# A two-layer early-fusion transformer: exponentials taken straight from the score banks in the second layer

## What is computed

```python
# second layer, attention (x is the normed h, 69 x 256 for each sample)
scores = einsum('bhqd,bhkd->bhqk', q, k) * 16 ** -0.5
scores = where(causal, scores, -inf)
weights = softmax(scores, axis=-1)
h = h + einsum('bhqk,bhkd->bhqd', weights, v) @ c_proj_w + c_proj_b
# second layer, feed-forward (x is the normed h again)
y = bit_linear(x, w1)                 # 256 -> 1024, per-token scale 127/max|x|, rounded
y = silu(depthwise_conv1d(y))         # three taps along the tokens
h = h + bit_linear(y, w2)             # 1024 -> 256, per-token scale from max|y|, rounded
```

## Time and profile before

| | |
|---|---|
| device time, median of 3 runs | 857.08 us (856.58 to 857.84) |
| the profiled execution | 857.1 us, its span on the core 855.3 us |
| PE busy in the span | 754.5 us (88%) |
| DVE busy | 596.7 us (70%) |
| ACT busy | 439.1 us (51%) |
| POOL busy | 381.2 us (45%) |
| granted TensorE clock, mean | 0.932 |

### The profile page before, as it was taken

How to read it: one execution, slowest core, us unless ns; L and a number is a source line. 1 busy time by engine, 2 the same in 40 slices (tenths; PEclk the granted TensorE clock), 3 DMA queues, 4 the chain that set the end, 5 groups by cost and what they waited for, 6 DMA issues and landing times.

```text
span 855.3 us, 20374 instructions
## 1 busy us (share of the span) xinstructions
PE 754.5 (88%) x6953; PEld 667.5 (78%) x6953; DVE 596.7 (70%) x1446; ACT 439.1 (51%) x1047; POOL 381.2 (45%) x515
## 2 busy tenths in 40 slices
PE   4999999999999961999993999999999999999533
PEld 4999999999999950676663998888888888888322
DVE  0467777767777747222221358999999999999893
ACT  1444554444454431222221567777777777776551
POOL 1434545445545542222204676666666666652000
PEclk8999999999999975899996899999999999999755
DMA  5365321000000422222210000000000000000000
GB/s 172 97 250 214 59 61 24 12 9 9 8 14 10 155 17 48 45 68 62 69 51 20 7 15 9 7 16 15 15 16 15 16 15 17 16 9 11 7 7 14
DMA packets 23983, 36.41 MB, mean 43 GB/s; under 512 B 10038, under 2 KB 21211, under 8 KB 23115
## 3 DMA queue, kind: packets, MB, share of 16 engines
q1 hardware_dynamic: 14474, 26.20, 10.8%
q0 software_dynamic: 5808, 5.63, 3.1%
q10 hardware_dynamic: 3600, 3.28, 1.1%
HBM read 27.21 MB, written 7.88 MB: 41 GB/s over the span
## 4 chain that ended last, share of the span: by engine, by line
PE 57%; DVE 24%; issue 11%; DMA 4%; ACT 2%; POOL 1%; SPq 1%; DVEq 0%; ACTq 0%; POOLq 0%
PE bank_h L1494 5%; PE bank_d L1494 4%; PE bank_f L1468 4%; PE bank_e L1468 4%; PE bank_b L1456 4%; PE bank_g L1479 4%; PE bank_e L1649 3%; PE bank_c L1505 3%; PE bank_c L1667 3%; PE bank_c L1445 3%; PE bank_f L1649 2%; DVE diff L908 2%; PE bank_d L1667 2%; DVE w L1207 2%; PE bank_a L1445 2%
## 5 line engine op out<-in xcount | busy, mean ns | idle before, releaser
L466 POOL TENSOR_TENSOR qbd<-qt,consts_f 128x560 f32<-128x560 f32 x128 | 163.8, 1286 | 186.2 <-PE bank_e L1468 94.9
L615 ACT ACTIVATE pt<-bank_g 69x448 f32<-69x448 f32 x128 | 69.3, 541 | 35.5 <-PE bank_h L1479 34.1
L609 ACT ACTIVATE prob<-diff 112x345 f32<-112x345 f32 x128 | 62.0, 485 | 38.7 <-DVE diff L908 38.7
L1494 PE MATMUL bank_h<-values,pt 69*69 69x68 f32 x1024 | 74.5, 226 | 2.2 <-ACT pt L624 2.2
L1468 PEld LDWEIGHTS bank_e<-kt,qbd 128*112 128x112 f32 x640 | 71.7, 179 | 1.4
L1494 PEld LDWEIGHTS bank_d<-values,pt 69*69 69x69 f32 x1024 | 70.5, 143 | 2.2
L1468 PEld LDWEIGHTS bank_f<-kt,qbd 128*112 128x112 f32 x640 | 72.1, 180 | 0.0
L1494 PEld LDWEIGHTS bank_h<-values,pt 69*69 69x69 f32 x1024 | 70.0, 142 | 2.6 <-ACT pt L615 2.5
L1479 PE MATMUL bank_g<-consts_f,prob 112*69 112x112 f32 x512 | 71.9, 263 | 0.0
L1494 PE MATMUL bank_d<-values,pt 69*69 69x68 f32 x1024 | 71.8, 226 | 0.0
L1468 PE MATMUL bank_f<-kt,qbd 128*112 128x69 f32 x640 | 71.7, 260 | 0.0
(11 more groups left out here) (208 smaller groups left out, 1877.3 us busy)
## 6 DMA issues: line engine op xcount, KB each, us to landing
w<-in_w SPq DMA_DIRECT2D x2, 4096.0 KB, 14.4
patches<-in_patches SPq DMA_DIRECT2D x16, 222.0 KB, 2.6
expert_results<-prob ACTq DMA_DIRECT2D x25, 128.0 KB, 1.9
expert_rows<-x SPq DMA_DIRECT2D x16, 138.0 KB
out<-h SPq DMA_DIRECT2D x16, 138.0 KB
f_raw<-in_f SPq DMA_DIRECT2D x2, 1024.0 KB, 8.5
patches<-in_b SPq DMA_DIRECT2D x1, 2048.0 KB, 9.6
wqkv<-in_wqkv SPq DMA_DIRECT2D x2, 768.0 KB
```

Of the source, the lines that this page charges most:

```text
L466: pool.tensor_tensor(qbd[u % 2][:], q.broadcast_to([128, NG, HPB, QG]), head_mask.unsqueeze(1).unsqueeze(3).broadcast_to([128, NG, HPB, QG ...
L609: act.activation(prob[u % 2][:], diff[u % 2][:], ACT.Exp, scale=DH ** -0.5).then_inc(S["prob_made"], 1)
L615: act.activation(pt[u % 2][:, :, 0:4, :].rearrange("t h g q -> t g h q"), banks["g"][0:T, 0:4 * SR].rearrange("t (g h q) -> t g h q", g=4, ...
L1494: ins = mm(heads_out[b][:, hd * (DH + 1):(hd + 1 + AHEAD) * (DH + 1)], pt[u % 2][:, i, :, :].rearrange("k g q -> k (g q)")[:, 0:T], values ...
```

## The change

Four things change, nearly all in the second layer.

1. **Sign.** `head_mask` carries -1/4 in place of 1 and the mask +1e30 in place of -1e30, in both layers, so the banks hold the scores negated and scaled. DVE takes the row minimum in place of the maximum (`row_min`, the same instruction with another operation), and the exponential's scale is -1. The first layer keeps `shift_scores` and one exponential of 345 columns.
2. **No shift in the second layer.** `shift_scores` is gone there. `exp_rows` takes the place of `exp_scores`: ACT reads the bank itself, one instruction for each of the five query groups, with that group's row minimum as per-partition bias. Group g covers only its causal keys, 14, 28, 42, 56 and 69 columns. The bank is free, and PE's `turn_p` may start, when the last of the five is done.
3. **Zeros.** Columns of `prob` beyond the causal ones are no longer written, so DVE clears both `prob` tiles once between the layers, after the last expert rows are stored; the first exponential waits for that.
4. **Orders.** The four bodies of the second layer are written in other orders with other lags (largest lag 7 in place of 6 on PE and DVE, 4 in place of 3 on POOL), and `BANKS1` with them. PE's instructions are the same in kind and number, and so are all others but those named above.

```diff
+            def exp_rows(p, u):
+
+                bank = "ef"[u % 2]
+                act.wait_ge(S["min_made"], UNITS * p + u + 1)
+                wait(act, S["p_turned"], UNITS * p + u - 1)
+                if p == 0 and u == 0:
+                    act.wait_ge(prob_cleared, 2)
+                sc = banks[bank][0:SR, 0:NG * T].rearrange("r (g k) -> r g k", g=NG)
+                for g in range(NG):
+                    n = min(T, QG * (g + 1))
+                    ins = act.activation(prob[u % 2][:, g, 0:n], sc[:, g, 0:n], ACT.Exp,
+                                         scale=-1.0, bias=rowmin[:, u % 2, g:g + 1])
+                ins.then_inc(BK[bank], 1)
...
-                dve.tensor_reduce(rowmax[:, u % 2, :], sc, X, ALU.max).then_inc(S["max_made"], 1)
+                dve.tensor_reduce(rowmin[:, u % 2, :], sc, X, ALU.min).then_inc(S["min_made"], 1)
...
+            for k in range(2):
+                dve.wait_ge(y_stored[k], 16 * ((TILES - k + 1) // 2))
+                dve.memset(prob_t[k][0:SR, :], 0.0).then_inc(prob_cleared, 1)
...
-                if live(s, 2, PAIRS):
-                    shift_scores(s - 2, 0)
-                    row_max(s - 2, 1)
...
             def turn_p(p, u):
-                pe.wait_ge(S["prob_made"], UNITS * p + u + 1)
+                if S is LS[0]:
+                    pe.wait_ge(S["prob_made"], UNITS * p + u + 1)
+                else:
+                    bank_is_moved("ef"[u % 2], f"scores{u}", p)
...
-            steps(pe, PAIRS, 6, body1)
+            steps(pe, PAIRS, 7, body1)
...
-    head_mask=_p[:, None] // DH == np.arange(HPB)[None, :],
+    head_mask=-(DH ** -0.5) * (_p[:, None] // DH == np.arange(HPB)[None, :]),
```

291 lines of the change are left out of this document (145 added, 146 removed).

## The result

The changed kernel takes 861.65 us (median of 7 runs, 860.47 to 864.55) beside 857.08 for the kernel before on the same chip (median of 7 runs, 855.75 to 861.17): ratio 1.0057, 95% interval 1.0036 to 1.0078. It is 0.6% slower where 1.3% faster was forecast, and outside the range. Its profiled execution took 862.7 us, 5.6 more than that of before.

A forecast was written before the change was run, and what follows sets the result against it. DVE was taken as the bound (21.05 of 21.09 us a step), PE close behind. Terms +1.5 - 2.3 - 9.4 - 2.0 + 1 = -11.2 us from 857.1 gave 845.9, say 846.0 us, 1.3% faster; range 842 to 853.5.

The forecast's parts named there:

- DVE loses the shifts: Second layer: four shifts a pair go, 1.8 us, so DVE's step falls to 19.3 us, under PE's floor by 0.8.
- the ten steps: Pairs 3 to 13: each step 0.94 us shorter at 20.15, together -9.4 us (ends -10.1 and -7.0).
- if POOL's spread queries run late: Condition in the rival that orders don't quite fit: step 20.5 to 20.9 us, 849.3 to 853.3 us, chance 0.17.
- no gain: Rival: waits held by DVE's shifts turn up elsewhere, as in the scores chain; step 21.0 to 21.1, 857 us, chance 0.07.
- PE's floor of 20.1: Full step: PE needs 20.1 us once its two waits for DVE are gone, so PE is late next.
- 0.9 a unit: ACT's five short exponentials take 0.9 us per unit, making 18.6 us a pair (17.8 to 20.2), under PE's 20.1.
- The start: Up to the first projection: 2.1 us delay plus about 1 allowance less 1.7 given back, +1.5 us (ends 0 and +4).
- Pairs 0 to 3: Steps between their projections: PE's work listed at 52.3 us in place of 54.6, so -2.3 us (ends 0 and -3).
- a PE with more gaps: Allowance of about 1 us for the delay at the first scores, with no row for it.
- Pairs 13 to 15: Between their add_projected: 19.8 plus 17.7, together 37.5 us in place of 39.5, so -2.0 us (ends -0.5 and -2.7).
- the drain: After pair 15's add_projected: 53.0 us before; left_tap ahead of scale_gated delays the output product, +1 us (ends -0.5 and +2).
- Slower: Rival that ACT becomes the bound: short exponentials don't overlap, ACT's step 22.4 us, about 872 us, chance 0.09.

The follow-up runs named there:

- pool_narrow: Changed kernel with POOL's mix and bias additions narrowed to 2 of 256 columns a batch, leaving out most of both sums; 844.92 us in one run.
- covered: fitted with DVE's x_diagonal and z_unscale moved up behind x_round, and variance2 with add_ffn put ahead of gate_hidden; 853.21 us, ratio 0.9968.
- mix_narrow: Changed kernel with only POOL's mix narrowed to 2 of 256 columns of each sample; 853.07 us in one run.
- before_narrow: Kernel before with POOL's mix and bias additions narrowed to 2 of 256 columns; 855.09 us in one run.
- small_moved: Changed kernel with DVE's x_unscale moved right behind x_scale, and z_step and x_step ahead of right_tap; 855.28 us, ratio 0.9975.
- fitted: bias_later with DVE's add_right and x_round moved behind add_projected and the row minimum of unit 2; 858.25 us, ratio 1.0027.
- bias_later: small_moved with POOL's bias addition moved from the start of its step to behind the gather of expert results; 851.39 us, ratio 0.9952.
- before_provoked: Kernel before with POOL's bias addition moved up right behind the gather of expert results; 877.13 us in one run.

## Why the prediction was wrong, point by point

**DVE loses the shifts, its step falls to 19.3.** This is the step that failed, and not in its arithmetic. DVE's own work did fall, to 19.0 (pool_narrow). But the durations were taken from rows of the kernel before, and the new orders gave three of those operations another neighbour on POOL: 2.4 us a step. So the ten steps came out at +3.3 where -9.4 was forecast. The prediction asked of the orders only what each item waits for by semaphore. It checked POOL for lateness ("if POOL's spread queries run late"), not for what runs on DVE beside it. That an idle engine's work can be a cost to the bound engine was in none of its rivals: "no gain" came near in time, 857, with a mechanism (the chain of scores) that no run shows. What stands ahead of the prediction says that the engines meet only at semaphores; DVE and POOL meet here without one. (A slip without weight: the ten steps between projections are 21.09 on the mean, but go from 21.06 to 21.23.)

**PE's floor of 20.1** was right: 20.02 with the short additions, 19.93 in covered. The gain of ten steps that it promised was 9.4; pool_narrow has 200.2 us for the ten, 10.7 less than before.

**ACT** was right: 0.9 a unit, ACT 18.9 in a step of after with everything, against 18.6. The Trainium skill, page ScalarE: Activation LUTs, section What ACT_TABLE_LOAD costs, makes 1.1 a unit by its rule (the prediction's estimate); the trace has 0.91. The clearing lay inside DVE's idle time, as said.

**The start** was right in its first two parts; its sum cannot be judged from one profile. The first norm starts at 462.49 (462.3 was worked out), `move_xt` at 464.78 (464.6). But the first projection came at 491.73. Stretches of before and after in that place:

```profile
472.00:480.00 8.00, 7.90 (x48) 7.91 (x49) 2.08 (x4) 3.45 (x10) 3.56 (x4) 0.57 0.07 18
```

```profile
472.00:480.00 8.00, 8.00 (x81) 7.39 (x80) 2.67 (x6) 7.10 (x28) 6.03 (x7) 1.00 0.01 2
```

Before, PE ran at a clock of 0.57 there, after at 1.00; so a faster PE made up for the delay of 2 us. That is no effect of the new orders that could be counted on: mix_narrow and pool_narrow have the same orders as after, and there the clock was 0.63 and 0.69 in this stretch and the first projection came at 495.67 and 494.20. And before_narrow has the orders of the kernel before, a clock of 1.00 there, and its first projection at 491.00. With a low clock in this stretch the kernels with new orders have it between 494.2 and 496.3, near the forecast's 496.

**Pairs 0 to 3:** -2.3 forecast, +5.0 measured. The list of PE's work was too short by 1.3 to 1.8 us, as pool_narrow (53.6, -1.0) and covered (54.1, -0.5) show with the clock at 1.00, where 52.3 was forecast. The rest is the low clock, for which the prediction had an allowance at the start ("a PE with more gaps") and nowhere else. It followed two PE waits of 0.84 and 0.85 us. The second is for the diagonal, which stood on DVE behind an `x_unscale` held for 1.0 us at 528. In small_moved `x_unscale` is short there, but `add_right` is held in its place (2.17), and PE waits 0.85 us for the diagonal as well; its other wait is 0.21, the clock stays at 1.00 and the three pairs take 54.2. So it is not shown that the hold-up brought the low clock. Against it speaks that in before_narrow, where DVE's operations ahead of the wait have their bare times, pairs 0 to 3 took 58.7 us with the same low clock. In both stretches its clock is much like that of after; up to pair 3 it takes 549.74 us and after 551.35, so with like clocks these two terms together cost 1.6 us, where -0.8 was forecast.

**Pairs 13 to 15** (-2.0) and **the drain** were right: between the additions of the two projections 37.56 us passed, where 37.5 was added up, and from the last addition of the projection to the end it took 53.9 us, where 54 was forecast. What the table has beyond +1 is the addition itself, which the new DVE order puts 0.9 us later behind its projection.

Together: the ten steps missed by 12.7 us, pairs 0 to 3 by 7.3, the end by 0.9, the start by -4.1; 16.8 us between -11.2 and +5.6. The ten steps are the part that the experiments explain; how the low clock divides the 7.3 and the -4.1 differs between executions.

**Chances.** Slower had 0.09, all of it on ACT. The case that happened was not among them.

## What to carry to other kernels

When operations are moved, look at each pair of neighbours in time on DVE and POOL, not only at semaphores: an SBUF-to-SBUF operation of POOL wants to stand beside reductions and reads of a bank on DVE. Moving one operation out of a hold-up can leave the next one in it, as in small_moved and fitted; take away the POOL operation's length first (as in pool_narrow, which computes less) to learn what all of them cost together. And look in more than one profile at where the low clock falls before you put a gain or a loss of a few us at the start down to an order. And an order that is best in the full steps can be wrong in the drain, where it may be written differently.

## What the hardware showed beyond that

A `tensor_scalar` on 69x2 elements was held for 1.0 us, and one `TENSOR_TENSOR` for 0.9 (bias_later) to 1.5 us (before_provoked). The last is more than POOL's whole 1.28, though by the records `add_left` had started 0.38 us ahead of the bias; whether an operation that has started can be held, or whether its record starts before it does, is open. The sentence of the Trainium skill (page SBUF — State Buffer, section Who interferes with whom) that the order of issue decides who blocks fits the rows after, where `mix` waits for `add_left` and then holds `x_unscale`, but not plainly this one.

The low clock came after PE waits, but no amount of waiting tells them apart: from 532 to 536 PE was busy 2.31 of 4 us after, and the clock fell; before it was busy less and the clock stayed (first row). In before_narrow, with the same orders as before, the same wait of 1.89 us for the heads in bank d ended at 531.77, and the clock fell (last two rows):

```profile
532.00:536.00 4.00, 2.11 (x26) 1.93 (x25) 4.00 (x10) 2.41 (x9) 3.51 (x5) 1.00 0.00 0
```

```profile
532.00:536.00 4.00, 4.00 (x35) 3.91 (x35) 2.60 (x4) 3.07 (x8) 1.80 (x4) 0.61 0.00 0
536.00:540.00 4.00, 4.00 (x22) 3.25 (x21) 3.60 (x12) 2.87 (x8) 1.18 (x4) 0.53 0.00 0
```

PE at that wait, before and in before_narrow:

```profile
535.14 0.47 PE L1701 MATMUL bank_d<-diag,consts_f 69*128 69x138 f32 x2 [1.89 <-DVE on L1249]
```

```profile
531.77 0.47 PE L1701 MATMUL bank_d<-diag,consts_f 69*128 69x138 f32 x2 [1.89 <-DVE on L1249]
```

What makes the difference stays open. It is worth 4 to 5 us a time: 25.03 us from pair 2 to 3 after, 25.14 in fitted and 24.38 in before_narrow, against 20.23 before. The times of the kernel before look the same way, though only their mean clocks are on record: of its 19 executions beside small_moved, twelve lie between 853.39 and 856.71 us with a mean clock of 0.930 to 0.936, and seven between 859.32 and 860.34 with 0.927 to 0.930. The seven of the changed kernel lie between 860.47 and 864.55, so how much of its 0.6% is the steps, and how much the share of executions with such a stretch, is not settled.
